# Attention part of an image network: three projections and the centring as groups of four 64x64 matmuls, images regrouped between partition halves, queues in a new order

## What is computed

```python
# layer 1, for every pixel; c = 64 channels, 8 images, 8 heads of 8
xn = groupnorm(x) * gn_g + gn_b
t  = xn @ ciw.T + cib + pe[image]                  # "t"
tn = layernorm(t) * ln1g + ln1b
q2, k2, v2 = (tn @ wq.T + bq) @ wiq.T + biq, ...   # "qkv"
attn = softmax_over_images(q2 . k2 / sqrt(8))
z  = (attn @ v2) @ wout.T + bout                   # "out projection"
t  = z + t                                         # z1 in the kernel
tn2 = layernorm(t) * ln2g + ln2b                   # "centring", variance
a  = tn2 @ w1.T + b1
g  = t @ w2.T + b2
t  = (a * gelu(g)) @ w3.T + b3 + t
out = t @ cow.T + cob + x                          # last projection
# layer 2
for _ in range(3):
    h = relu(conv3x3(out, w1) + b1)
    out = out + (conv3x3(h, w2) + b2) / 3
out = relu(out)
```

## Time and profile before

| | |
|---|---|
| median of 3 runs | 1245.43 us (1243.92 to 1246.52) |
| the profiled execution | 1244.47 us, of which the span is 1242.5 |
| PE busy in the span | 1147.9 us, 92% |
| DVE | 1104.6 us, 89% |
| ACT | 648.7 us, 52% |
| POOL | 417.1 us, 34% |
| mean granted TensorE clock | 0.986 of full |
| DMA over the span | 28 GB/s |

### The profile page before, as it was taken

How to read it: one execution, slowest core, us unless ns; L and a number is a source line. 1 busy time by engine, 2 the same in 40 slices (tenths; PEclk the granted TensorE clock), 3 DMA queues, 4 the chain that set the end, 5 groups by cost and what they waited for, 6 DMA issues and landing times. The chain is left out here.

```text
span 1242.5 us, 20220 instructions
## 1 busy us (share of the span) xinstructions
PE 1147.9 (92%) x6594; PEld 625.4 (50%) x6594; DVE 1104.6 (89%) x1521; ACT 648.7 (52%) x1518; POOL 417.1 (34%) x384
## 2 busy tenths in 40 slices
PE   3169999999999999999998899999999999999995
PEld 2156766766766776776763333333333333333331
DVE  4648999999999999999995799999999999999995
ACT  1356787787777777777763224233323422342422
POOL 3112313312322322322321344444444453455440
PEclk9989999999999999999999899999999999999998
DMA  8010111111101101101000000030001100030003
GB/s 300 18 33 18 33 29 27 35 27 29 30 25 34 25 25 34 25 25 35 18 13 14 1 1 1 1 63 5 1 1 29 40 2 1 1 68 1 1 1 68
DMA packets 87508, 35.34 MB, mean 28 GB/s; under 512 B 70209, under 2 KB 86850, under 8 KB 86930
## 3 DMA queue, kind: packets, MB, share of 16 engines
q1 hardware_dynamic: 85634, 33.81, 10.3%
q0 software_dynamic: 768, 0.33, 0.1%
q10 hardware_dynamic: 1040, 0.35, 0.1%
HBM read 26.09 MB, written 8.39 MB: 28 GB/s over the span
## 5 line engine op out<-in xcount | busy, mean ns | idle before, releaser
L1012 PE MATMUL acc<-mixed,cwp 128*128 128x512 f32 x768 | 354.8, 607 | 4.0 <-DVE mixed L1073 2.5
L1012 PEld LDWEIGHTS acc<-mixed,cwp 128*128 128x128 f32 x768 | 139.7, 191 | 217.8 <-issue 214.5
L1030 ACT ACTIVATE y<-acc,cols 128x1024 f32<-128x1024 f32 x96 | 111.8, 1210 | 249.2 <-PE acc L1022 249.2
L769 POOL TENSOR_TENSOR rstd<-var,half 128x8 f32<-128x8 f32 x32 | 80.2, 2507 | 382.0 <-DVE var L733 382.0
L1022 PE MATMUL acc<-mixed,cwp 64*64 64x512 f32 x1536 | 184.2, 600 | 11.4 <-POOL mixed L1073 11.4
L485 DVE TENSOR_TENSOR prod<-qkv 128x1024 f32<-128x1024 f32 x128 | 155.7, 1218 | 3.9 <-DVE qkv L675 1.5
L495 DVE TENSOR_TENSOR prod<-attn,qkv 128x1024 f32<-128x1024 f32 x128 | 153.2, 1216 | 0.0
L521 PE MATMUL b<-consts,prod 128*128 128x128 f32 x1024 | 139.1, 281 | 1.2 <-DVE prod L485 1.0
L1072 POOL TENSOR_TENSOR mixed<-xs 128x256 f32<-128x256 f32 x92 | 83.0, 902 | 156.7 <-DVE xs L1061 156.7
L1038 DVE TENSOR_TENSOR y<-y,acc 128x512 f32<-128x512 f32 x192 | 120.5, 679 | 15.6 <-ACT y L1030 15.6
L540 PE MATMUL b<-consts,prod 128*128 128x128 f32 x1024 | 128.8, 273 | 0.8 <-DVE var L733 0.3
(11 more groups left out here) (165 smaller groups left out, 1612.7 us busy)
## 6 DMA issues: line engine op xcount, KB each, us to landing
xs<-in_x SPq DMA_DIRECT2D x4, 2048.0 KB, 16.5
xa<-in_x SPq DMA_DIRECT2D x32, 256.0 KB, 2.7
xr<-in_x SPq DMA_DIRECT2D x64, 128.0 KB, 2.8
out_y<-xs SPq DMA_DIRECT2D x32, 256.0 KB, 4.7
cw<-in_L_conv_w POOLq DMA_DIRECT2D x2, 144.0 KB, 4.1
consts<-in_consts ACTq DMA_DIRECT2D x1, 192.0 KB
group<-in_consts SPq DMA_DIRECT2D x1, 64.0 KB
w1n<-in_L_conv_w ACTq DMA_DIRECT2D x1, 64.0 KB
```

The source lines that it names most:

```text
L1012: pe.matmul(psum[PSUM_PAIR[v, q, j]][i][:, :, :], weights(v, i, j).rearrange("p n o -> p (n o)"), mixed[v][i][:, s0:s0 + WIDE, j, :], star ...
L1030: act.activation(pairs(y[i][q][:, :, :]), m1, ACT.Identity, bias=cols[:, (6, 8)[v]:(7, 9)[v]]).then_inc(m1_out[i][q], 1)
```

## The change

- **Images regrouped.** In tt, z, z1 and what follows, the lower partition half now holds images 0 to 3 and the upper 4 to 7; the 128-column block 2e+j of half d holds image 4d+2j+e. The input xa still comes in the old pairing, so `pe_t` moves the images across.
- **Groups of four.** `pe_t`, `pe_z1`, `pe_center` and the cowT part of `pe_out` (now `pe_cow`) issue matmuls with 64x64 weights, one for each quarter of the array: two groups of four with 128 columns for t, one group of four with 256 columns for each of the others. Input half and output half differ in two of the four, and the two input halves write to two different PSUM banks. Before, t, z1 and centring were whole-array matmuls with block-diagonal weights, and cowT two groups of two.
- **`pe_var2`** multiplies by 2 columns of the averaging matrix, not by 128.
- **PSUM.** t goes to a part of q_ps, z1 to both banks of zb (b6 and b3 together), centring to both of cb (b4 and b2). gel and gated are one buffer each for both halves; each `dve_gated` now covers half the columns of both.
- **Order.** All five lists are in a new order, with other semaphores. On POOL and DVE the second layernorm's rstd2 and tn2 come one iteration earlier in the list; max comes one earlier, away from shift; z comes early in ACT's list.
- **No counted loop**: all 35 iterations are written out.

The diff, cut:

```diff
-            link(dve.tensor_tensor(top["tcol"][:, :], pt[0][:, 0:PAIRS], pet[:, :], ALU.add))
+            for e in range(2):
+                link(dve.tensor_tensor(top["tcol"][:, 2 * e:2 * e + 2], pt[e][:, 0:2], pet[:, 2 * e:2 * e + 2], ALU.add))
...
         def pe_t(pe, t, k):
 
             wait_loaded(pe, xa_in, t, k)
-            wait(pe, tn2_done, t - 3)
-            for p in range(PAIRS):
-                m = pe.matmul(b2[:, TILE * p:TILE * (p + 1)], top["resT"][:, p, :], xa[k % 2][:, p, :], start=True, stop=True)
+            wait(pe, raw_out[1], t)
+            for j in range(2):
+                for e in range(2):
+                    for d in range(2):
+                        m = pe.matmul(q_ps[half(d), e, 0, TILE * j:TILE * (j + 1)], top["resT"][half(e), 2 * d + j, half(e)],
+                                      xa[k % 2][half(e), 2 * d + j, :], start=True, stop=True)
             m.then_inc(t_mm, 1)
 
         def pe_qkv(pe, t, k, g):
             wait(pe, t_out, t + 1)
-            wait(pe, raw_out, 2 * t + g)
+            if g == 0:
+                wait(pe, t_out, t + 1)
+            else:
+                wait(pe, raw_out[0], t + 1)
             for p in range(2):
-                for e in range(2):
-                    half = slice(C * e, C * e + C)
-                    m = pe.matmul(q_ps[:, e, p, :], tt[k][half, TILE * (2 * g + p):TILE * (2 * g + p + 1)],
-                                  top["basis"][half, :], start=True, stop=True)
-            m.then_inc(qkv_mm, 1)
+                for d in range(2):
+                    m = pe.matmul(q_ps[:, d, p, :], tt[k][half(d), TILE * (2 * g + p):TILE * (2 * g + p + 1)],
+                                  top["basis"][half(d), :], start=True, stop=True)
+            m.then_inc(qkv_mm[g], 1)
 
...
+            wait(pe, shift_done, upto(t + 2))
             wait(pe, gelu_out[0], t)
-            pe.matmul(b6[:, :], top["woutT"][:, :], z[:, :], start=True, stop=True).then_inc(z1_mm, 1)
+            for e in range(2):
+                for d in range(2):
+                    m = pe.matmul(zb[half(d), e, 0:HALF], top["woutT"][half(e), half(e)],
+                                  z[half(e), HALF * d:HALF * (d + 1)], start=True, stop=True)
+            m.then_inc(z1_mm, 1)
 
         def pe_center(pe, t, k):
             wait(pe, z1_out, t + 1)
+            wait(pe, tn2_done, t)
             wait(pe, z_out, t + 1)
-            pe.matmul(b4[:, :], center, z1[k % 2][:, :], start=True, stop=True).then_inc(cen2_mm, 1)
+            for d in range(2):
+                for e in range(2):
+                    m = pe.matmul(cb[half(e), d, 0:HALF], center[half(d), half(d)],
+                                  z1[k % 2][half(d), HALF * e:HALF * (e + 1)], start=True, stop=True)
+            m.then_inc(cen2_mm, 1)
 
         def pe_g(pe, t, k):
             wait(pe, z1_out, t + 1)
-            wait(pe, shift_done, upto(t + 2))
             wait(pe, z1_out, t + 1)
-            for e in range(2):
-                half = slice(C * e, C * e + C)
-                pe.matmul((b6, b3)[e][:, :], top["w2T"][half, :], z1[k % 2][half, :], start=True, stop=True).then_inc(g_mm, 1)
+            wait(pe, z1_out, t + 1)
+            for d in range(2):
+                pe.matmul((b6, b3)[d], top["w2T"][half(d), :], z1[k % 2][half(d), :], start=True, stop=True).then_inc(g_mm, 1)
 
         def pe_var2(pe, t):
             wait(pe, sq2_out, t + 1)
             wait(pe, sq2_out, t + 1)
             wait(pe, cen2_out, t + 1)
             for p in range(PAIRS):
-                m = pe.matmul(b4[:, P * p:P * (p + 1)], sq2[:, TILE * p:TILE * (p + 1)], cmean, start=True, stop=True)
+                m = pe.matmul(b4[:, 2 * p:2 * p + 2], sq2[:, TILE * p:TILE * (p + 1)], cmean[:, ::C], start=True, stop=True)
             m.then_inc(var2_mm, 1)
 
         def pe_rstd2(pe, t):
...
         def rows(ap, r):
 
-            return ap.rearrange("p (q r w) -> p r q w", q=PAIRS, r=2)[:, r]
+            return ap.rearrange("p (e j r w) -> p r j e w", e=2, j=2, r=2)[:, r]
 
         def out_of(e, r):
 
             return (b5, b7)[e][C * r:C * r + C, 0:PAIRS * HW]
 
-        def pe_out(pe, t, k, e):
-            wait(pe, gated_done[e], t + 1)
-            half = slice(C * e, C * e + C)
+        def pe_out(pe, t, d):
+            for e in range(2):
+                wait(pe, gated_done[e], t + 1)
             for r in range(2):
-                pe.matmul(out_of(e, r), top["w3T"][:, :], rows(gated[e][:, :], r), start=True, stop=False)
-            for r in range(2):
-                m = pe.matmul(out_of(e, r), top["cowT"][half, :], rows(z1[k % 2][half, :], r), start=False, stop=True)
-            m.then_inc(out_mm[e], 1)
+                m = pe.matmul(out_of(d, r), top["w3T"][:, :], rows(gated[:, N * d:N * (d + 1)], r), start=True, stop=False)
+            m.then_inc(out_mm[d], 1)
+
+        def pe_cow(pe, t, k):
+            for d in range(2):
+                for r in range(2):
+                    m = pe.matmul(out_of(d, r), top["cowT"][half(d), :], rows(z1[k % 2][half(d), :], r), start=False, stop=True)
+            m.then_inc(cow_mm, 1)
 
         def act_t(act, t, k):
             wait(act, t_mm, t + 1)
             wait(act, z1_out, t - RING + 1)
-            wait(act, qkv_mm, 2 * (t - RING + 1))
-            for p in range(PAIRS):
-                pair = slice(TILE * p, TILE * (p + 1))
-                m = act.activation(tt[k][:, pair], b2[:, pair], ACT.Identity, bias=top["tcol"][:, p:p + 1])
+            for g in range(2):
+                wait(act, qkv_mm[g], t - RING + 1)
+            for e in range(2):
+                for j in range(2):
+                    blk = 2 * e + j
+                    m = act.activation(tt[k][:, TILE * blk:TILE * (blk + 1)], q_ps[:, e, 0, TILE * j:TILE * (j + 1)],
+                                       ACT.Identity, bias=top["tcol"][:, blk:blk + 1])
             m.then_inc(t_out, 1)
 
...
-            if tiles[1]:
-                pe_scores_t(pe, t - 1, 0)
             if tiles[3]:
                 pe_var2(pe, t - 3)
             if tiles[1]:
+                pe_scores_t(pe, t - 1, 0)
                 pe_scores_t(pe, t - 1, 1)
-            if tiles[0]:
-                pe_qkv(pe, t, k, 1)
-            if tiles[1]:
-                pe_scores_t(pe, t - 1, 2)
             if tiles[2]:
                 pe_av(pe, t - 2, 0)
             if tiles[1]:
+                pe_scores_t(pe, t - 1, 2)
                 pe_scores_t(pe, t - 1, 3)
-            if tiles[2]:
-                pe_av(pe, t - 2, 1)
-                pe_av(pe, t - 2, 2)
+            if tiles[0]:
+                pe_qkv(pe, t, k, 1)
             if tiles[3]:
                 pe_rstd2(pe, t - 3)
             if tiles[1]:
                 pe_scores(pe, t - 1)
             if tiles[2]:
-                pe_av(pe, t - 2, 3)
+                pe_av(pe, t - 2, 1)
             if tiles[3]:
                 pe_a(pe, t - 3)
             if tiles[2]:
+                pe_av(pe, t - 2, 2)
+                pe_av(pe, t - 2, 3)
+            if tiles[3]:
+                pe_out(pe, t - 3, 0)
+            if tiles[2]:
                 pe_z1(pe, t - 2)
             if tiles[3]:
-                pe_out(pe, t - 3, (k - 3) % RING, 0)
-                pe_out(pe, t - 3, (k - 3) % RING, 1)
+                pe_out(pe, t - 3, 1)
+                pe_cow(pe, t - 3, (k - 3) % RING)
 
         def act_iteration(act, t, k, tiles):
+            if tiles[2]:
+                act_exp(act, t - 2)
+            if tiles[3]:
+                act_z(act, t - 3)
             if tiles[1]:
                 act_scale(act, t - 1, (k - 1) % RING)
-            if tiles[2]:
-                act_exp(act, t - 2)
             if tiles[0]:
                 act_t(act, t, k)
             if tiles[3]:
                 act_square2(act, t - 3)
                 act_centered(act, t - 3)
+                act_gelu(act, t - 3, 1)
             if tiles[0]:
                 act_squares(act, t, 0)
                 act_raw(act, t, k, 0)
             if tiles[3]:
-                act_gelu(act, t - 3, 0)
+                act_rrep(act, t - 3)
+            if tiles[1]:
+                act_scores_t(act, t - 1)
             if tiles[0]:
                 act_squares(act, t, 1)
             if tiles[3]:
-                act_rrep(act, t - 3)
-                act_gelu(act, t - 3, 1)
-            if tiles[1]:
-                act_scores_t(act, t - 1)
+                act_gelu(act, t - 3, 0)
             if tiles[0]:
                 act_raw(act, t, k, 1)
-            if tiles[2]:
-                act_z(act, t - 2)
 
         def dve_iteration(dve, t, k, tiles):
             if tiles[0]:
                 dve_var1(dve, t)
+            if tiles[1]:
+                dve_shift(dve, t - 1)
             if tiles[2]:
                 dve_p2(dve, t - 2, (k - 2) % RING, 3)
             if tiles[3]:
-                dve_tn2(dve, t - 3)
-            if tiles[1]:
-                dve_max(dve, t - 1)
```

(88 more changed lines are left out.)

65 lines of the change are left out of this document (37 added, 28 removed).

## The result

The changed kernel takes 1210.71 us, median of 4 runs (1210.25 to 1212.51); the kernel before took 1244.68 in the runs beside it. The ratio is 0.9729, interval 0.9712 to 0.9746: 34 us less. The profiled execution has a span of 1208.4 us, against 1242.5. The forecast was 1208, the range 1202 to 1226.

What follows compares the result with a forecast made beforehand. PE's stream was taken to bound the kernel at 18.43 us per tile, DVE next. 28 x (18.43 - 17.2) = 34.4, plus 3 for filling and draining, less 0.2 setup, is 37: 1245.4 - 37 = 1208 us, range 1202 to 1226.

Steps and rivals of the forecast that it cites:

- Price of a group of four: PE's t, centring, z1 and cow: as groups of four they save 0.56, 0.43, 0.49 and 0.60 us per tile.
- Rival B: Groups of four on PE are held up by weight loads and save little: 1238 to 1244 us; chance 0.04.
- var2 costs the same: PE's var2 with 2 moving columns stays unchanged from 0.90 us, since loading 128 weight columns sets the pace.
- Rival C: PE's var2 gets short, 0.2 to 0.3 us, and DVE's 17.05 alone counts: 1204 us; chance 0.05.
- PE's sum of 16.35: PE's work per tile after the change: 18.43 less the four savings of the groups, 16.35 us.
- The walk: Steps through one tile's new order at period 17.1, with 0.3 us for shape changes in PE's stream.
- The limit by DVE, 17.05: DVE's work per tile without its waits for PE, 17.05 us, capping the gain at 1.38 per tile.
- The ring: Chain from p2's part 3 over av, z, scale, tt, centring, var2 back to av: about 17.15 us; 17.2 per tile taken.
- Rival A: The ring is longer than walked, through late weight loads: 17.5 to 18.1 per tile, 1217 to 1234 us; chance 0.24.
- The order as mere placing: The new order of the queues has no gain or cost of its own in the forecast sum.
- Filling and draining: The three tiles of filling and two of draining together become 3 us shorter, an estimate.
- Clock (rival D): PE falls to the lower clock in the attention part, making the kernel slower than before; chance 0.05.

Runs made afterwards that it cites:

- v2: The kernel before with the new queue orders and straight code, but its whole-array matmuls, cowT groups of two and old layout kept: 1255.5 us.
- v3: The changed kernel with var2 multiplying by all 128 columns of the averaging matrix, as before: 1211.0 us.
- v4: The changed kernel with part 2 of p2 computing one of two images from the second tile on, DVE 0.54 us less per tile: 1210.8 us.
- v6: The changed kernel with t's two groups of four issued twice, 0.44 us more PE work per tile: 1222.7 us.
- v9: The changed kernel with part 3 of p2 put ahead of shift on DVE: 1210.7 us.
- v11: The changed kernel with part 3 of p2 moved ahead of tn2 on DVE: 1211.5 us.
- v14: v9 with PE's first part of av moved behind the second transposition: 1214.8 us.
- v1: The changed kernel's groups of four, layout and straight code with all five queue orders of the kernel before: 1261.6 us.
- v8: The changed kernel with DVE's max of the first two tiles put behind the next tile's var1: 1213.7 us.

## Why the prediction was right, and where it wasn't

- **PE's stream bounds the kernel before, DVE is next**: right. The even period and DVE's waits for PE said so, and in v2, where PE keeps its old work, DVE still waits for it.
- **Price of a group of four**: right. 0.56, 0.43, 0.49 and 0.60 forecast, 0.56, 0.41, 0.45 and 0.68 measured: 2.08 against 2.10. The conv part's rows were a good price list. Rival B is out.
- **var2 costs the same**: right (v3). Rival C is out.
- **PE's sum of 16.35**: wrong by 0.5. PE's stream is 17.20 - 0.32 = 16.88. The terms of the groups were right; what was missing is that the new order costs PE about 0.3 by itself (18.74 in v2 against 18.43). In the changed kernel 0.33 of the 0.5 stand in av (3.92 against 3.59), 0.12 in qkv's first group and var2 together, and 0.05 each at rstd2 and between g and qkv. The walk, which had 0.3 for changes of shape, was nearer. It did no harm because the sum was not what bound.
- **The limit by DVE, 17.05**: right in size, no more than that. Less its wait at tn2, DVE needs 17.07 (17.20 - 0.13), and its instructions kept their lengths (tn2 0.69, the pair of gated 1.40 against 1.41). But v4 shows that the changed kernel is not bound by it.
- **The ring**: the length was right (17.15 walked, 17.2 with the slip at tn2), the ring wasn't. I walked from p2 over ACT and named tn2's 0.1 as a slip beside it. tn2's wait for rstd2 is a link of the ring that binds. Its other link I passed over: by the walk PE reaches part 1 of the scores' transposes at 8.5 + 1.0 + 0.9 = 10.4, just when DVE ends part 1 of p1 (9.2 + 1.2), and I wrote "without a stop". Rival A, a period above 17.5, didn't come. The number came out because several rings lie within 0.1 to 0.2 of each other, as v6, v9, v11 and v14 show. So 17.2 was right partly by luck.
- **The order as mere placing**: wrong. The prediction priced the order at nothing. Groups alone are 17 us slower than before, order alone 11 slower, both together 34 faster (v1, v2). I had seen that gated's halves merge and that out waits for both, but costed it in the new order only.
- **Filling and draining**: 3 us less forecast, 0.7 more measured, with filling 1.9 longer. This term is larger than the whole miss of the median, 1208 against 1210.7; the rest of the account is half a microsecond in the steady tiles and small gains in the setup and the conv part. v8 didn't find the cause.
- **Clock (rival D)**: it stayed at the upper level through the steady part.

## What to carry over

When two engines both work at over 90%, shortening one buys only the distance to the next loop, so write down every loop through the queues, not one; a wait of 0.1 us that looks like a slip may be the loop that binds. Merging work of two halves into one group makes consumers of the first half wait for the second: price it together with the place of these consumers in their queue, here 35 us for one item. A path that closes always adds up to the period; look for the waits on it, down to 0.1 us inside a row, to see whether it is the one that binds. To find what binds in a finished schedule, put a small known piece of work in one place, or take one out, and read where the waiting moves to; a busy share of 99% proves nothing (v4).

## What the runs showed of the hardware

Four 64x64 matmuls of only 128 columns run at once as well as those of 512 columns: t's 16 passes are over in 0.44 us, 0.11 for each four. A matmul pass with 2 moving columns behind 128 fresh weight columns takes as long as one with 128, 0.11 us (the changed kernel and v3). In filling, where PE stands idle for some us at a time (4.08 ahead of 74.46, 4.68 ahead of 90.31), part of its work runs at a lower clock. PE's matmuls of the changed kernel in that stretch:

```profile
76.47 5.60 PE L535 MATMUL cb<-consts,prod 128*128 128x128 f32 x32
...
92.31 2.79 PE L535 MATMUL cb<-consts,prod 128*128 128x128 f32 x16
...
95.81 1.91 PE L535 MATMUL cb<-consts,prod 128*128 128x128 f32 x16
```

The same 16 transposes take 2.79 us and then 1.91, and 32 take 5.60, where 4.01 do in v14's steady part. The granted clock averages 0.91 from 75 to 90 us and 0.87 from 90 to 105, between its two levels, and 1.00 from 300 to 400.
